# Graph-network megakernel: a table stage without GpSimd, and the first layer's normalising cut into four chunks

## The reference

```python
x = layernorm(x + L0(x))   # two GCN layers: segment_sum((x @ W)[src], dst) + b, ReLU between them
x = layernorm(x + L1(x))   # an edge network: silu(silu([x[src], x[dst], dist] @ eW1) @ eW2), summed by src, node MLP
x = layernorm(x + L2(x))   # messages: relu features of the neighbour and relu(edge_w * W2), summed by src, @ W4
x = layernorm(x + L3(x))   # polynomial of degree 10 in the normalised adjacency
def layernorm(x): m = mean(x); v = var(x); return (x - m) / sqrt(v + 1e-5)
```

## Time and profile before

| | us |
|---|---|
| median of the runs (lowest, highest) | 1601.18 (1600.2, 1608.76) |
| profiled execution: its own time | 1603.67 |
| profiled execution: span | 1601.5 |
| PE busy / DVE busy / ACT busy / POOL busy | 1395.6 / 1232.4 / 594.9 / 44.4 |
| mean granted PE clock | 0.961 of full |

### The profile page before, as it was taken

How to read it: one execution, slowest core, us unless ns; L and a number is a source line. 1 busy time by engine, 2 the same in 40 slices (tenths; PEclk the granted TensorE clock), 3 DMA queues, 4 the chain that set the end, 5 groups by cost and what they waited for, 6 DMA issues and landing times. The chain is left out here.

```text
span 1601.5 us, 44020 instructions
## 1 busy us (share of the span) xinstructions
PE 1395.6 (87%) x16795; PEld 1291.0 (81%) x16795; DVE 1232.4 (77%) x3606; ACT 594.9 (37%) x1073; POOL 44.4 (3%) x82
## 2 busy tenths in 40 slices
PE   0745468879987999999999979699999999999997
PEld 0434456669986888888888849599999999999997
DVE  4999988865446888888888867667777687677676
ACT  0249779971105777777777740100000000000000
POOL 2111100000000000000000000000000000000000
PEclk9989989989998999999999979689999999999999
DMA  1000035541005445454232260000000000000000
GB/s 20 9 1 0 0 91 157 158 129 33 2 15 152 127 133 153 114 152 114 83 106 75 63 152 2 6 2 2 2 2 2 2 2 2 2 2 2 2 6 19
DMA packets 37008, 83.91 MB, mean 52 GB/s; under 512 B 22941, under 2 KB 23957, under 8 KB 36863
## 3 DMA queue, kind: packets, MB, share of 16 engines
q1 hardware_dynamic: 33617, 81.46, 18.2%
q10 hardware_dynamic: 3024, 0.39, 0.2%
q0 software_dynamic: 224, 0.13, 0.1%
HBM read 60.76 MB, written 21.14 MB: 51 GB/s over the span
## 5 line engine op out<-in xcount | busy, mean ns | idle before, releaser
L1835 PE MATMUL L_psA<-L_parts,mat 125*128 125x192 bf16 x6250 | 517.1, 246 | 0.0
L1835 PEld LDWEIGHTS L_psA<-L_parts,mat 125*128 125x128 bf16 x6250 | 515.5, 98 | 1.0 <-DVE L_parts L1912 0.8
L1241 PEld LDWEIGHTS L_ps_pre<-L_drow,mat 128*128 128x128 bf16 x2250 | 128.8, 98 | 30.3 <-issue 1.1
L1774 ACT COPY L_wk<-L_Wk 128x64 f32 (+1 forms) x10 | 1.9, 242 | 391.6 <-PE L_psA L1835 391.6
L1899 DVE TENSOR_REDUCE L_sumr<-L_psA 125x64 f32<-125x192 f32 x225 | 80.5, 358 | 70.9 <-PE L_psA L1835 70.5
L1241 PE MATMUL L_ps_pre<-L_drow,mat 128*128 128x32 bf16 (+3 forms) x2250 | 133.1, 213 | 0.0
L690 PE MATMUL ps_count<-onehot 128*128 128x125 bf16 x1200 | 106.8, 218 | 17.0 <-DVE onehot L653 9.5
L1430 DVE TENSOR_TENSOR L_e<-L_e,mat 128x512 f32<-128x512 f32 x125 | 86.2, 689 | 39.2 <-ACT L_e L1328 39.2
L653 DVE TENSOR_TENSOR onehot<-iota_bf,codes 128x1024 bf16<-128x1024 bf16 x150 | 100.7, 688 | 17.9 <-PE ps_count L690 16.7
L891 PE MATMUL L_psA<-L_gparts,mat 125*128 125x192 bf16 x1250 | 109.3, 247 | 0.2 <-DVE L_sumr L995 0.2
L690 PEld LDWEIGHTS ps_count<-onehot 128*128 128x128 bf16 x1200 | 86.8, 98 | 25.1 <-DVE onehot L653 15.3
(11 more groups left out here) (314 smaller groups left out, 2279.4 us busy)
## 6 DMA issues: line engine op xcount, KB each, us to landing
L_drow<-rows_d SPq DMA_DIRECT2D x25, 728.0 KB
mat<-m_d SPq DMA_DIRECT2D x25, 684.2 KB
mat<-rows_d SPq DMA_DIRECT2D x25, 640.0 KB, 4.3
m_d<-panel SPq DMA_DIRECT2D x13, 684.2 KB
m_d<-xb SPq DMA_DIRECT2D x12, 684.2 KB
L_drow<-rows_d SPq DMA_DIRECT2D x25, 84.5 KB
mat<-m_d SPq DMA_DIRECT2D x25, 79.4 KB
m_d<-panel SPq DMA_DIRECT2D x13, 79.4 KB
```

Source lines behind the costliest of these rows:

```text
L1241: last = nc.tensor.matmul(ps_pre[bank][:, to:to + n], w, drow[k][:, of:of + n], start=False, stop=(r == 2 and cc == pieces[-1][0]))
L1835: last = nc.tensor.matmul(ps[:, 0:3 * D], t.mat[0:B, kb, b * B:b * B + P], parts[src][:, kb].rearrange("p r d -> p (r d)"), start=(kb == 0 ...
```

## The change

It has three parts.

1. **Table stage.** POOL has no work there: its two `tab` copies go to ACT, and the fill of row 6 of `wparts` goes to the constants in the first block of the program. DVE packs `dense` first and copies `over` behind it; the two casts to `src1` and `dst1` go to ACT, behind its copies from PSUM. The mask `minus` is gone: a negative weight is picked by `is_lt`, as a positive one is by `is_gt`, which leaves its sign as it is; so the message layer multiplies the second number of `we` by -1.
2. **First layer, second spreading.** `bn_aggr` of a block follows its `bn_stats` at once, with a wait between them. Subtraction, root, reciprocal and multiplication are done in four chunks of blocks, (0, 8), (8, 16), (16, 23) and (23, 25). A chunk is scaled in the iteration two blocks after its last block; the third therefore in the iteration of block 24, and the fourth behind the loop.
3. **Message layer.** The multiplication by -1 stands between the reduction and the two copies before PE's release, with a wait for the reduction.

```diff
@@ place_edges, first block, gpsimd
                 nc.gpsimd.memset(off_bf[:, :, NB], 0.0)
+                nc.gpsimd.memset(t.wparts[:, 6, :], 1.0)
@@ edge_tables, vector
-                v.tensor_copy(over[:, 0:DUP * NB].rearrange("p (r b) -> p r b", b=NB), parts_of[:, 0, :, NB, :])
-                v.tensor_copy(over[:, DUP * NB:], parts_of[:, 1, 0, NB, :]).then_inc(overs, 1)
...
                 last.then_inc(packed, 1)
-                v.tensor_copy(by_col(t.src1[:]), field[0])
-                v.tensor_copy(by_col(t.dst1[:]), field[1])
-                v.tensor_scalar(by_col(minus[:]), w[0], 0.0, -1.0, ALU.is_lt, ALU.mult).then_inc(done, 1)
+                v.tensor_copy(over[:, 0:DUP * NB].rearrange("p (r b) -> p r b", b=NB), parts_of[:, 0, :, NB, :])
+                v.tensor_copy(over[:, DUP * NB:], parts_of[:, 1, 0, NB, :]).then_inc(overs, 1)
                 for r in range(3):
                     v.scalar_tensor_tensor(wv(r), w[0], 0.0, w[r], ALU.is_gt, ALU.mult)
-                dve.wait_ge(done, 1)
-                for r in range(3):
-                    v.tensor_tensor(wv(3 + r), by_col(minus[:]), w[r], ALU.mult)
+                    v.scalar_tensor_tensor(wv(3 + r), w[0], 0.0, w[r], ALU.is_lt, ALU.mult)
@@ edge_tables, gpsimd
-                for f in (3, 4):
-                    nc.gpsimd.tensor_copy(tab[:, f - 1], field[f]).then_inc(pool_tabbed, 1)
-                nc.gpsimd.memset(t.wparts[:, 6, :], 1.0)
@@ edge_tables, scalar
-                for f in (1, 2):
+                for f in (1, 2, 3, 4):
                     nc.scalar.copy(tab[:, f - 1], field[f]).then_inc(tabbed, 1)
...
                 nc.scalar.copy(t.over_rows, ps[3][0:B, NB - held[3][0], :])
+                nc.scalar.copy(by_col(t.src1[:]), field[0])
+                nc.scalar.copy(by_col(t.dst1[:]), field[1])
@@ gcn_layers, scalar
-                roots(nc, act, c, mv, std, var, root)
+                for i, blocks in enumerate(chunks):
+                    act.wait_ge(var, i + 1)
+                    nc.scalar.activation(std[:, blocks], mv[:, blocks, 1], ACT.Sqrt, bias=c.eps[0:B, :]
+                                         ).then_inc(root, 1)
@@ gcn_layers, vector
+                def take_stats(b):
+                    S(nc.vector.bn_stats(bn[:, b, :], y[:, b, :]))
+                    S.wait()
+                    last = nc.vector.bn_aggr(mv[:, b, :], bn[:, b, :])
+                    if b in ends:
+                        last.then_inc(var, 1)
+                    else:
+                        S(last)
+                def scale_rows(i):
+                    blocks = chunks[i]
+                    some = [B, blocks.stop - blocks.start, D]
+                    dve.wait_ge(var, i + 1)
+                    S(nc.vector.tensor_tensor(y[:, blocks], y[:, blocks], mv[:, blocks, 0:1].broadcast_to(some),
+                                              ALU.subtract))
+                    dve.wait_ge(root, i + 1)
+                    S(nc.vector.reciprocal(rstd[:, blocks], std[:, blocks]))
+                    S.wait()
+                    nc.vector.tensor_tensor(t.xb[:, blocks], y[:, blocks], rstd[:, blocks].unsqueeze(2).broadcast_to(
+                        some), ALU.mult).then_inc(xb, 1)
...
                     if b >= 1:
-                        S(nc.vector.bn_stats(bn[:, b - 1, :], y[:, b - 1, :]))
-                    if b >= 2:
-                        S(nc.vector.bn_aggr(mv[:, b - 2, :], bn[:, b - 2, :]))
+                        take_stats(b - 1)
+                    if b >= 2 and b - 2 in ends:
+                        scale_rows(ends.index(b - 2))
                 dve.wait_ge(y2, NB)
-                normalize(nc, dve, S, y, bn, mv, std, rstd, t.xb, var, root, NB - 1, NB - 2
-                          ).then_inc(xb, 1)
+                take_stats(NB - 1)
+                scale_rows(len(chunks) - 1)
@@ message_layer, vector
                 S(v.reduce_sum(we[:], t.wsum[:, :, 0:6].rearrange("p b (s r) -> p b s r", r=3), X))
+                S.wait()
+                S(v.tensor_scalar(we[:, :, 1], we[:, :, 1], -1.0, None, ALU.mult))
                 dve.wait_ge(g_ps, 1)
```

More of the change, by code:

```diff
@@ L465, in edge_tables @@
         sem = lambda n: s.enter_context(nc.semaphore(n))
-        minus = sb("minus", [P, NT], F32)
         ps = [s.enter_context(nc.psum_tensor(f"ps_row{i}", [P, 8, P], BF16)) for i in range(4)]
@@ L469, in edge_tables @@
         tab = sb("tab", [P, 4, NC, NB], BF16)
-        done, overs, packed, tabbed, pool_tabbed, rowed = map(sem, (
-            "table_step", "overs", "packed", "tabbed", "pool_tabbed", "rowed"))
+        overs, packed, tabbed, rowed = map(sem, ("overs", "packed", "tabbed", "rowed"))
         held = ((0, 5), (5, 13), (13, 21), (21, NC))
@@ L499, in _ @@
                 last.then_inc(packed, 1)
-                v.tensor_copy(by_col(t.src1[:]), field[0])
-                v.tensor_copy(by_col(t.dst1[:]), field[1])
-                v.tensor_scalar(by_col(minus[:]), w[0], 0.0, -1.0, ALU.is_lt, ALU.mult).then_inc(done, 1)
+                v.tensor_copy(over[:, 0:DUP * NB].rearrange("p (r b) -> p r b", b=NB), parts_of[:, 0, :, NB, :])
+                v.tensor_copy(over[:, DUP * NB:], parts_of[:, 1, 0, NB, :]).then_inc(overs, 1)
                 for r in range(3):
                     v.scalar_tensor_tensor(wv(r), w[0], 0.0, w[r], ALU.is_gt, ALU.mult)
-                dve.wait_ge(done, 1)
-                for r in range(3):
-                    v.tensor_tensor(wv(3 + r), by_col(minus[:]), w[r], ALU.mult)
-            @block.gpsimd
-            def _(pool):
-                for f in (3, 4):
-                    nc.gpsimd.tensor_copy(tab[:, f - 1], field[f]).then_inc(pool_tabbed, 1)
-                nc.gpsimd.memset(t.wparts[:, 6, :], 1.0)
+                    v.scalar_tensor_tensor(wv(3 + r), w[0], 0.0, w[r], ALU.is_lt, ALU.mult)
             @block.tensor
@@ L524, in _ @@
                         elif i < NB:
-                            pe.wait_ge(*((tabbed, f) if f < 3 else (pool_tabbed, f - 2)))
+                            pe.wait_ge(tabbed, f)
                             some = tab[:, f - 1, 5 * j:5 * j + 5, :].rearrange("p c b -> p (c b)")
@@ L866, in gcn_layers @@
         y = t.xa
+        chunks = [slice(lo, hi) for lo, hi in ((0, 8), (8, 16), (16, 23), (23, NB))]
         with nc.Block() as block:
@@ L1005, in _ @@
                 dve.wait_ge(xb, 1)
+                ends = [blocks.stop - 1 for blocks in chunks]
+                def take_stats(b):
[17 more added lines that the diff above has]
+                        some), ALU.mult).then_inc(xb, 1)
                 for b in range(NB):
```

## The result

| | kernel before | changed kernel |
|---|---|---|
| median (lowest to highest) of 20 runs each, same chip | 1603.57 (1600.07 to 1609.15) | 1600.59 (1598.61 to 1604.54) |
| profiled execution: own time, span, the time around the span | 1603.67, 1601.55, 2.1 | 1600.31, 1595.89, 4.4 |
| mean granted clock of that execution | 0.961 | 0.962 |

The ratio is 0.9977, 95% interval [0.9966, 0.9988]: 3.7 us faster by it, 2.98 by the medians. I had forecast 1594.9 with a range up to 1598.8, and the time lies outside it. The span became 5.7 us shorter (6.25 forecast), but own time minus span grew by 2.3 us.

The account below looks back on a forecast made before the run. PE, busy 1395.6 of 1601.5 us, bounds the kernel; gains come only where it stands and another engine ends a block. -4.85 - 1.75 + 0.1 + 0.25 = -6.25 gave 1597.4, on the median's scale 1594.9; range 1591.3 to 1598.8.

Parts of the forecast that it names:

- The step that failed: Final conversion: 6.25 less than own time 1603.67 gives 1597.4, then 2.5 off for the median of 1601.18, giving 1594.9.
- DVE in the table stage: Table stage: dropped instructions win 2.08 us, narrow copies without POOL 2.77; DVE's end moves 4.85 earlier.
- The two rivals on it: Table stage: narrow copies slow by themselves (-4.0, 1597.2, chance 0.1); gain passed on to nothing (-1.4, 1599.8, chance 0.09).
- ACT's casts: Table stage end: src1 and dst1 casts take 1.4 us each, bounds 0.7 and 2.11; ACT ends 0.7 ahead of DVE.
- The boundary: After the table stage: the next block starts its own work 0.67 us after DVE's end, as before.
- Normalising: End of first layer: tail of 3.9 us becomes 2.2; 1.75 won, bounds 1.2 and 2.1.
- Chunks 1 and 2: Second spreading, first layer: each costs DVE 1.6 us in one iteration, made up one block later; nothing reaches PE.
- The clock at that boundary: First layer's end: rival that PE resumes before its clock falls, transposes some 1.2 us less; -7.5, 1593.7, chance 0.2.
- Message layer: Before PE's release: waiting for the reduction plus one small instruction puts +0.25 us on the path, bounds 0.1 and 0.4.
- The memset in the first block: First block: POOL's memset could hold DVE's first cast at 4.89 by 0 to 0.6 us; +0.1 taken.
- The slower rival: Preparation and message layer products: half clock comes back later behind moved stretches; +11, net +4.8, 1606, chance 0.05.

Follow-up runs that it names:

- e6: Kernel before with four more never executed ACT instructions in the fallback for unsorted edges; ratio 1.0004, 3.88 us around the span.
- e9: Changed kernel with DVE instead of ACT copying turned rows in the never executed fallback, ACT's program 141 instructions shorter; median 1597.65, ratio 0.9971, around 2.08.
- e18: Kernel before with one never executed ACT instruction repeated 16 more times; 2.00 us around the span.
- e5: Kernel before with ten more never executed DVE instructions in the fallback for unsorted edges; ratio 0.9999, 2.13 us around the span.
- e7: Kernel before with only POOL's two tab copies moved to ACT, order and memset as before; ratio 1.0009, around 3.54.
- e11: Changed kernel with two one-element GpSimd memsets of an unused tile added in the first block; median 1601.25, ratio 0.9976, around 4.76.
- e3: Kernel before with only the four chunks of normalising in the first layer; ratio 0.9994, around 3.74.
- e1: The kernel before run again, with no edit; ratio 1.0001.

## Why the prediction was wrong, point by point

- **The step that failed** is the last: "Its own time is 1603.67 (span 1601.5, 2.2 around it): 1597.4. That run was 2.5 above the median of 1601.18, so on the scale of the median 1594.9." Both halves of it. The time around the span is no constant of the kernel: it went from 2.1 to 4.4 in the two profiled executions, and e6, e9 and e18, with e5 beside them, show that it follows ACT's code, executed or not. The extra time lies behind the last instruction. And 2.5 us were taken off for a median of three runs; over 20 runs it is 1603.57, so the profiled execution was an ordinary one and nothing was to be taken off.
- With both mended the sum closes: 1603.67 - 6.25 + 0.59 (span) + 2.30 (around) = 1600.31, the profiled execution's own time. That part is bookkeeping, and what each part was is below. On the medians it is 1603.57 - 6.25 + 2.5 = 1599.8 against 1600.59; the last 0.8 is within the scatter.
- **DVE in the table stage**: -4.85 forecast, -4.95 measured. The two rivals on it fell: the narrow copies take 0.26 and 0.18, e7 frees them without touching their pattern, and the gain reached the next block. ACT's casts took 1.46 where I took 1.4 (bounds 0.7 and 2.11), and ACT ended 1.26 before DVE, not 0.7.
- **The boundary** "0.67 after DVE's end as now" was 1.07. The step so gave 4.55. e11 shows that it is the barrier's release, which two more GpSimd instructions far ahead bring back to 0.08.
- **Normalising**: -1.75 forecast, -1.93 measured, inside its bounds. Chunks 1 and 2 reached no PE instruction.
- **The clock at that boundary**: the rival had PE resume ahead of the fall, and it did, by 0.1 us. But the rival held the fall fixed at 475.96, and it moved: in all twenty traces it comes 2.4 to 4.0 us behind the last add. It came all the same, and only its end came earlier; the transposes gained 0.42 where the rival had 1.2. The half clock lasts 3.4 us in the eight traces in which PE restarts ahead of the fall or at most 0.1 behind it, and 6.8 in the twelve in which it restarts 0.8 or more behind it. Among these are e3 and e11, with the chunks and the same 3.39 to PE's restart: their transposes take 5.49, so the 0.42 is not won in every execution. With it, 2.34 were won here from the last add to the products behind the transposes.
- **Message layer**: +0.25 forecast, +0.21 measured. The terms as priced give -4.55 - 1.93 + 0.21 = -6.27 beside the forecast -6.25: the misses cancel, which is luck.
- **The memset in the first block**: +0.1 taken, nothing measured (DVE's first cast at 4.82, before at 4.89).
- **Chance**: +2.24 ahead of the table stage (0.50 of it before the early dip), -1.0 in the edge network (452.5 instead of 453.5 from its first product behind the transposes to the reduction of `wsum`; the other traces show 452.4 to 453.5). With -4.55, -2.34 and +0.21 this is -5.44 of the -5.66; the rest is +0.1 between the table stage and the last add and -0.3 behind the message layer's reduction. The slower rival (the clock comes back later behind the moved stages) was seen in no trace at its price; in e3 and e11, where the half clock lasts 6.8, the first 16 products behind the transposes take 2.19 and 2.28 instead of 1.95.
- Pooled, 136 executions of before and 30 of changed have median spans of 1602.2 and 1596.1: 6.1 shorter, beside 6.25 forecast. This agreement proves less than it seems: the shortest tenth of the spans ends at 1598.3 and 1594.5, 3.8 apart, and the longest tenth begins at 1606.6 and 1598.3, 8.3 apart. Why the changed kernel's spans scatter less no run shows.

## What to carry to other kernels

Forecast span and own time apart, and look at own time minus span of every run: here an edit that lengthened ACT's code by a few instructions gave back 2.5 us there, also when they never ran, and a kernel that is tuned to tenths should be tried with its unexecuted code laid out in another way. Take no correction of a few us from a median of three where the lowest and the highest are 8 us apart. Where a narrow DVE copy ends just when a GpSimd instruction does, price it by what it takes without GpSimd: 0.26 and 0.18 us here in place of 1.52 and 1.97.

## What the runs showed of the hardware that I had not expected

- Own time minus span: 2.0 to 2.2 us for some lengths of ACT's program, 3.5 to 4.9 for others, not monotone, and all of the difference behind the last instruction; ten more instructions of DVE or two of GpSimd do not move it (2.13 with e5; 4.76 beside 4.61 with e11).
- The release of one barrier took 0.47 us instead of 0.08 in kernels with two GpSimd instructions fewer, and 0.08 again with two more far ahead of it.
- One and the same kernel has spans from 1597.6 to 1607.2, with a mean granted clock of 0.963 below 1600 and 0.958 above 1605: falls to the half clock of 3.4 us at 57, 262, 272 and 334 us stand in e1's profiled execution and not in the first one.
- The half clock behind PE's stand at the end of the first layer lasted 3.4 us where PE restarted ahead of the fall or within 0.1 us of it, and 6.8 where it restarted 0.8 or more behind it.
